# A fused expert MLP and prefix-softmax pooling kernel: the last batch's attention tail reordered, W's exponentials moved to ScalarE, and a batch's exponentials put in one place

## The chip, the cores and the metric

The kernel runs on one core of a Trainium2 chip. The metric is device time in microseconds (us) of one execution. Engines are named as in the profile: PE is TensorE (PEld its weight loads), DVE is VectorE, ACT is ScalarE, POOL is GpSimd, SP is SyncE, which issues the DMAs.

## The reference

Four batches of 1024 rows by 512. First a layer with a shared and an expert part, then attention pooling over all rows of a batch with a mask that depends on the batch's type. Both are added to x:

```python
h = gelu(x @ fc1_w.T + fc1_b)                     # exact gelu, 2048 hidden
y = concat(h @ fc2_w.T + fc2_b, h @ experts_w[idx].T + experts_b[idx])
x = x + y
scores = tanh(x @ W1 + b1) @ v                    # per 512 rows as [B, S]
mask   = l <= j, l >= j or l != j                 # by type 0, 1, 2
p      = softmax(where(mask, scores[l], -1e30))   # over l, for each row j
x = x + (p @ x) / count(mask)                     # S = 1024 here
```

## The kernel before

x is held transposed, 128 rows of features by 512 tokens in a tile. Every product of full precision is made of three with operands split in a high and a low part (`three`, L764 to L767): ACT makes the high part (`hi`, L981), DVE subtracts it to get the low part (`lo`, L1263). fc1 of a batch runs as Strassen-like products P1 to P7 into the banks hA and hF, in eight steps p (0 to 7, two blocks of 128 hidden each), with fc2 (banks y) of its first 512 rows in between and three places k for other work. Then 16 steps u do fc2 of its second 512 rows.

There are three bodies: `first`, `loop` (run for batches 1 to 3, `b` in code) and `tail`. The attention of batch b-1 is done in the loop body of batch b, in pieces hung at the places (p, k) by the table `POST_P`; that of the last batch is the tail, after the last product of fc2. In the tail each engine goes through its tasks in an order written by hand: PE by `TAIL_ORDER`, ACT by `TAIL_ACT`, DVE by `TAIL_DVE`. Banks go round: two job banks j in the loop, all eight in the tail, a job taking the next one once its last reader has counted `bank_read` up. In a loop step DVE and ACT do the tasks of (p, 0) before they go on with the adds and gelus of the products; product P2 overwrites hF, and so waits for DVE's add of hF (L1458, semaphore `add_done`); the sequence on PE is P1, P5, P6, jobs, P3, P7, jobs, P2, P4, with groups of fc2 between.

The attention of a batch, by task:

- `xn` transposes x back, four tiles a half (L858); ACT copies the high part, DVE subtracts; in the tail ACT also makes a full copy (`full`, counted by `xfull_done`) that the output is added to.
- `attn` is the product with W1, tanh by ACT (L1106), `score` the product with v (L866), s in an 8x128 layout (8 chunks of 128 rows).
- `maxima` scans s from both sides (L1424, L1426), `stats` (L870 to L872) transposes and spreads them; `row_maxima` (L1431 to L1440) makes Ef, t88, mc and the row maxima m8, of which `mT` (L876) and `bc` (L882, two of 512 columns) spread the negated maxima over 128 partitions.
- DVE adds scores and masks to them: P (own chunk, L1333, four of 128x128) and W (other chunks, L1337, one of 128x512) for each half. ACT takes the exponentials of both in place (L1147), then the high parts Ph and Ws (L981), DVE the low parts Pl and a third of Ws (L1263).
- `expE` spreads exp(Ef) on the diagonals of E4 (L1345), `sums` multiplies E4 with all of x (L887, L888: 16 products) to Bs.
- `scan`, `total`, `den`, `rd` make the denominators, with POOL (L705 to L717) and the small exponentials `exps_B` and `exps_M`.
- `pool` c: three products with Ph and Pl (`own_chunk`) and one of Ws with Bs (L904), DVE scales and adds (L1399 in the tail), SP stores. In the tail the own chunks of 0 to 3 are made before `rd` (L895).

Six fill products (L948, `FILLS`) stand in the tail's wait before `mT`. The tasks `expPW`, `exp` and `PW` are the exponentials of P and W and their split. Waits on the full copies, before their banks are written again, come from one table:

```python
FULL_BEFORE = {("bc", 0): 1, ("bc", 1): 2, ("sums",): 3, ("rd", 0, CH): 4}
```

## Time and profile before

| what | value |
|---|---|
| median of 3 runs | 784.71 us (783.61 to 785.57) |
| the profiled execution's own time | 784.57 us |
| its span, first to last instruction | 782.8 us |
| PE, DVE, ACT, POOL busy | 770.2, 402.5, 387.0, 132.7 us |
| mean granted clock of PE | 0.995 |
| last product of fc2 starts | 749.65 us |

Times within the profile are microseconds from the span's start. Busy time of PE has modelled ends: products of 512 columns show 0.39 us each and start 0.23 us apart at full clock, so starts are to be compared, not ends. "Granted clock" is the share of full speed (2.4 GHz) that the throttle gave PE. Between the end of the last instruction and the profiled execution's own time lie 1.8 us that the change doesn't touch. A group such as `x4` in a timeline is four instructions merged into one row.

### The profile page before, as it was taken

The numbers are of one execution on the slowest core, as the hardware profiler recorded it, in microseconds if no ns is written. First come the engines' busy times: TensorE is split into PE (matmuls) and PEld (weight loads), VectorE is DVE, ScalarE is ACT, GpSimd is POOL, SyncE is SP. The second block draws the span as 40 slices with busy tenths as digits, with TensorE's granted clock in tenths as the row PEclk, the third lists the DMA queues.
The fourth block names the chain that finished last, engine by engine and source line by source line (L and its number), as shares of the span: only waits on it lengthen the run. The fifth ranks groups of instructions, "written<-read, shape, count | busy, mean of one in ns | idle before, by whom it ended". The sixth has DMA issues, their size and how long they took to land.

```text
span 782.8 us, 11478 instructions
## 1 busy us (share of the span) xinstructions
PE 770.2 (98%) x3462; PEld 626.9 (80%) x3462; DVE 402.5 (51%) x713; ACT 387.0 (49%) x665; POOL 132.7 (17%) x184
## 2 busy tenths in 40 slices
PE   9999999999999999999999999999999999999977
PEld 6788888888888888888888888888887888888865
DVE  6854667563445332754536433376245542255666
ACT  6856665443546433543546633446254653344552
POOL 3172221400011121410001022050001102114011
PEclk9999999999999999999999999999999999999998
DMA  6899998877854568867776466985787466787722
GB/s 215 281 346 330 307 338 271 268 228 231 236 190 149 175 204 280 259 202 239 225 228 188 147 209 216 284 253 178 232 252 219 144 194 207 223 284 208 228 67 108
DMA packets 130715, 176.93 MB, mean 226 GB/s; under 512 B 10064, under 2 KB 97632, under 8 KB 130656
## 3 DMA queue, kind: packets, MB, share of 16 engines
q1 hardware_dynamic: 130496, 176.20, 72.0%
q8 instruction: 29, 0.48, 0.2%
q14 instruction: 30, 0.25, 0.1%
q0 software_dynamic: 160, 0.01, 0.0%
HBM read 136.33 MB, written 39.85 MB: 225 GB/s over the span
## 4 chain that ended last, share of the span: by engine, by line
PE 95%; DVE 2%; ACT 1%; DMA 1%; issue 0%; SPq 0%; DVEq 0%; ACTq 0%
PE y L765 15%; PE y L767 15%; PE y L766 15%; PE hA L765 8%; PE hA L767 7%; PE hA L766 7%; PE hF L765 6%; PE hF L766 6%; PE hF L767 5%; PE j L858 2%; PE j L765 1%; PE j L767 1%; PE j L766 1%; PE j L866 1%; PE j L835 1%; PE j L834 1%
## 5 line engine op out<-in xcount | busy, mean ns | idle before, releaser
L765 PE MATMUL y<-hs,w2c 128*128 128x512 f32 x512 | 201.8, 394 | 0.2
L767 PE MATMUL y<-hs,w2c 128*128 128x512 f32 x512 | 199.6, 390 | 0.0
L766 PE MATMUL y<-hs,w2c 128*128 128x512 f32 x512 | 199.4, 389 | 0.0
L765 PEld LDWEIGHTS y<-hs,w2c 128*128 128x128 f32 x512 | 96.1, 188 | 22.1 <-DVE hs L1263 1.9
L767 PEld LDWEIGHTS y<-hs,w2c 128*128 128x128 f32 x512 | 96.1, 188 | 20.5
L766 PEld LDWEIGHTS y<-hs,w2c 128*128 128x128 f32 x512 | 96.2, 188 | 19.3
L765 PE MATMUL hA<-xch,w1c 128*128 128x512 f32 x252 | 100.0, 397 | 0.9 <-DVE xcl L1263 0.6
L767 PE MATMUL hA<-xch,w1c 128*128 128x512 f32 x252 | 98.6, 391 | 0.0
L766 PE MATMUL hA<-xcl,w1c 128*128 128x512 f32 x252 | 98.6, 391 | 0.0
L1035 ACT ACTIVATE hst<-hst,bcol 128x512 f32<-128x512 f32 x62 | 43.9, 721 | 85.3 <-DVE hst L1458 85.3
L1263 DVE TENSOR_TENSOR hs<-gb,hs 128x512 fp32r<-128x512 f32 x64 | 43.5, 716 | 65.1 <-ACT hs L981 65.1
L765 PE MATMUL hF<-xch,w1c 128*128 128x512 f32 x190 | 76.2, 401 | 0.3 <-issue 0.3
L766 PE MATMUL hF<-xcl,w1c 128*128 128x512 f32 x190 | 74.5, 392 | 0.0
L767 PE MATMUL hF<-xch,w1c 128*128 128x512 f32 x190 | 74.3, 391 | 0.0
L1263 DVE TENSOR_TENSOR hs<-hst,hs 128x512 fp32r<-128x512 f32 x64 | 44.6, 697 | 37.3 <-ACT hs L981 36.2
L981 ACT ACTIVATE hs<-hst 128x512 fp32r<-128x512 f32 x64 | 40.4, 631 | 47.2 <-PE y L767 46.8
L765 PEld LDWEIGHTS hA<-xch,w1c 128*128 128x128 f32 x252 | 47.5, 188 | 13.9 <-issue 1.9
L767 PEld LDWEIGHTS hA<-xch,w1c 128*128 128x128 f32 x252 | 47.6, 189 | 10.1
L766 PEld LDWEIGHTS hA<-xcl,w1c 128*128 128x128 f32 x252 | 47.6, 189 | 9.4
L755 POOL TENSOR_TENSOR x1T<-x1T,xnl 128x512 f32<-128x512 f32 x24 | 30.8, 1290 | 137.9 <-DVE x1T L1402 137.9
L1458 DVE TENSOR_TENSOR hst<-hF,hst 128x512 f32<-128x512 f32 x31 | 21.4, 691 | 56.4 <-PE hF L767 55.9
L1035 ACT ACTIVATE gb<-gb,bcol 128x512 f32<-128x512 f32 x31 | 22.4, 724 | 54.8 <-DVE gb L1458 54.7
(283 smaller groups left out, 1096.3 us busy)
## 6 DMA issues: line engine op xcount, KB each, us to landing
w2c<-w2s SPq DMA_DIRECT2D x114, 384.0 KB, 3.5
w1c<-w1s SPq DMA_DIRECT2D x24, 768.0 KB, 4.6
w2c<-exs SPq DMA_DIRECT2D x114, 128.0 KB, 4.0
w1c<-w1s SPq DMA_DIRECT2D x48, 256.0 KB, 3.5
w1c<-w1s SPq DMA_DIRECT2D x24, 512.0 KB, 4.1
x1T<-in_x SPq DMA_DIRECT2D x32, 256.0 KB, 5.6
w1s<-w1c SPq DMA_DIRECT2D x8, 768.0 KB, 4.4
w2s<-w2c SPq DMA_DIRECT2D x16, 384.0 KB, 4.5
```

What stands on the lines that cost most here:

```text
L755: nc.gpsimd.tensor_tensor(oo[:, c % OUTS, :], oo[:, c % OUTS, :], xnl[:, c, :].bitcast(f32), ALU.add).then_inc(row_sum, 1)
L765: nc.tensor.matmul(ps, ah, bh, start=first, stop=False, skip_group_check=onto)
L766: nc.tensor.matmul(ps, ah, bl, start=False, stop=False, skip_group_check=onto)
L767: return nc.tensor.matmul(ps, al, bh, start=False, stop=last, skip_group_check=onto)
L834: nc.tensor.matmul(bank[:, :], W1h[:, dc, :], xh[:, dc, :], start=dc == 0, stop=False)
L835: nc.tensor.matmul(bank[:, :], W1l[:, dc, :], xh[:, dc, :], start=False, stop=False)
L858: last = nc.tensor.transpose(bank[:, i * P:(i + 1) * P], x1T[:, i, c * P:(c + 1) * P], ident[:, :])
L866: last = nc.tensor.matmul(bank[0:CH, 0:P], vz[:, t * CT + i, :], th[t][:, i * P:(i + 1) * P], start=(i == 0), stop=(i == CT - 1))
L981: return nc.scalar.activation(out_, in_, ACT.Copy)
L1035: nc.scalar.activation(tile, hA[:, :] if order == 4 else tile, ACT.Gelu, bias=bcol[:, R_FC1 + m:R_FC1 + m + 1]).then_inc(gelu_done, 1)
L1263: return nc.vector.tensor_tensor(out_, in_, hi_.bitcast(f32), ALU.subtract)
L1458: nc.vector.tensor_tensor(tile, bank[:, :], tile, ALU.add).then_inc(add_done, 1)
```

## The change

- In the tail, `attn` goes ahead of xn 1, its tanh comes in two halves (own semaphore), the score product ahead of xn 3; `total` behind `sums`; one fill product fewer, and they don't wait for a full copy.
- The three operations of the row maxima that only need the own chunk (m0) go from `row_maxima` to `maxima`, that is from behind `stats` to ahead of it, in all batches; Ef behind mc. A new small operation makes Wb, the bias of W.
- DVE no longer adds W: ACT takes W's exponentials straight from the bank of bc, four of 128x128 a half with Wb as bias, into the same tile. The bank is then free when ACT has read it, not DVE.
- In a loop body both halves of the exponentials stand at (3, 0), where the second half stood at (4, 0); at (4, 0) only its split is left.
- In the tail, ACT and DVE do P and W apart, in a new order, and the last full copy is ACT's last task; the waits for full copies move.
- E4 gets 8 columns more so that the three casts to its diagonals become one.

The tables and PE's part:

```diff
-WARM, FILLS = 8, 6
+WARM, FILLS = 8, 5
...
-          (2, 2): [("mT",)], (3, 0): [("bc", 0), ("bc", 1), ("expE",), ("expB",), ("expM",), ("scan",), ("expPW", 0)],
+          (2, 2): [("mT",)], (3, 0): [("bc", 0), ("bc", 1), ("expE",), ("expB",), ("expM",), ("scan",), ("exp", 0), ("exp", 1), ("split", 0)],
           (3, 1): [("sums",), ("total",)], (3, 2): [("den",)],
-          (4, 0): [("rd", 0, BC), ("rd", BC, CH), ("expPW", 1)], (4, 1): [("pool", 0)], (4, 2): [("pool", 1)],
+          (4, 0): [("rd", 0, BC), ("rd", BC, CH), ("split", 1)], (4, 1): [("pool", 0)], (4, 2): [("pool", 1)],
...
-    ("xn", 0), ("xn", 1), ("attn",), ("xn", 2), ("xn", 3), ("score",), ("stats",), ("expE",), ("mT",), ("bc", 0), ("bc", 1),
-    ("scan",), ("total",), ("expPW", 0), ("expPW", 1), ("sums",), ("den",), ("rd", 0, CH)] + [("pool", c) for c in range(CH)]
+    ("xn", 0), ("attn",), ("xn", 1), ("xn", 2), ("score",), ("xn", 3), ("stats",), ("expE",), ("mT",), ("bc", 0), ("bc", 1),
+    ("scan",), ("split", 0), ("split", 1), ("sums",), ("total",), ("den",), ("rd", 0, CH)] + [("pool", c) for c in range(CH)]
...
-    ("xn", 0), ("xn", 1), ("attn",), ("xn", 2), ("xn", 3), ("full", 0), ("full", 1), ("expE",), ("expB",), ("full", 2), ("expM",),
-    ("full", 3), ("exp", 0), ("PW", 0), ("exp", 1), ("sums",), ("PW", 1)]
+    ("xn", 0), ("attn",), ("xn", 1), ("xn", 2), ("full", 0), ("xn", 3), ("expE",), ("full", 1), ("expB",), ("full", 2),
+    ("splitP", 0), ("expM",), ("splitW", 0), ("splitP", 1), ("sums",), ("splitW", 1), ("full", 3)]
...
-            ("xn", 1), ("score",), ("xn", 2), ("stats",), ("mT",), ("expE",), ("xn", 3), ("bc", 0), ("scan",), ("bc", 1),
-            ("expPW", 0), ("total",), ("sums",), ("expPW", 1), ("den",), ("rd", 0, CH)] + [("pool", c) for c in range(CH)]
-
-FULL_BEFORE = {("bc", 0): 1, ("bc", 1): 2, ("sums",): 3, ("rd", 0, CH): 4}
+            ("xn", 1), ("score",), ("xn", 2), ("stats",), ("mT",), ("expE",), ("bcP", 0), ("xn", 3), ("scan",),
+            ("loP", 0), ("bcP", 1), ("loW", 0), ("total",), ("sums",), ("loP", 1), ("den",), ("loW", 1), ("rd", 0, CH)] + [("pool", c) for c in range(CH)]
+
+FULL_BEFORE = {("bc", 0): 1, ("sums",): 2, ("total",): 3, ("pool", 0): 4}
...
-                    wait_used(pe, kind, b, at(kind, place, ("attn",)))
+                    if kind == "tail":
+                        pe.wait_ge(tanh_half, 1)
+                    else:
+                        wait_used(pe, kind, b, at(kind, place, ("attn",)))
                     if kind == "first":
                         pe.wait_ge(vz_done, 1)
                     for i in range(CT):
+                        if kind == "tail" and i == CT // 2:
+                            wait_used(pe, kind, b, at(kind, place, ("attn",)))
...
-                    wait_used(pe, kind, b, at(kind, place, ("xn", CT - 1)))
                     for c in range(CH):
+                        if c >= CT:
+                            wait_used(pe, kind, b, at(kind, place, ("xn", c - CT)))
...
 
                             idle = jb[bank_of(kind, at(kind, "p", ("bc", 1)))]
-                            pe.wait_ge(xfull_done, FULL_BEFORE["bc", 1])
                             for i in range(FILLS):
                                 nc.tensor.matmul(idle[:, :], W1h[:, 0, :], x1he[:, 0, :], start=True, stop=True)
...
                             pe.wait_ge(xfull_done, FULL_BEFORE[task])
 
                         for c in range(BC) if task[0] == "rd" else [task[1]] if task[0] == "pool" and task[1] >= BC else []:
+                            if ("pool", c) in FULL_BEFORE:
+                                pe.wait_ge(xfull_done, FULL_BEFORE["pool", c])
```

ACT's part:

```diff
-                    nc.scalar.activation(th[t], bank[:, :], ACT.Tanh, bias=bcol[:, R_B1:R_B1 + 1]
-                                         ).then_inc(bank_read[bank_of(kind, pos)], 1)
+                    if kind == "tail":
+                        mid = TT // 2
+                        nc.scalar.activation(th[t][:, 0:mid], bank[:, 0:mid], ACT.Tanh, bias=bcol[:, R_B1:R_B1 + 1]).then_inc(tanh_half, 1)
+                        nc.scalar.activation(th[t][:, mid:], bank[:, mid:], ACT.Tanh, bias=bcol[:, R_B1:R_B1 + 1]
+                                             ).then_inc(bank_read[bank_of(kind, pos)], 1)
...
-                    split_PW(kind, b, task[1])
+                    exp_P(b, task[1])
+                    exp_W(kind, b, place, task[1])
+                elif task[0] == "split":
+                    split_PW(kind, b, task[1], 0)
+                    split_PW(kind, b, task[1], 1)
+                elif task[0] == "splitP":
+                    exp_P(b, task[1])
+                    split_PW(kind, b, task[1], 0)
+                elif task[0] == "splitW":
+                    exp_W(kind, b, place, task[1])
+                    split_PW(kind, b, task[1], 1)
...
-            def exp_PW(kind, b, place, h):
+            def exp_P(b, h):
                 half = slice(h * TT, (h + 1) * TT)
-                wait_used(act, kind, b, at(kind, place, ("bc", h)))
-                for tile in (Pf, Wf):
-                    nc.scalar.activation(tile[:, half], tile[:, half], ACT.Exp).then_inc(exp_done, 1)
-
-            def split_PW(kind, b, h):
+                act.wait_ge(P_in, b * 2 + (h - 1))
+                nc.scalar.activation(Pf[:, half], Pf[:, half], ACT.Exp).then_inc(exp_done, 1)
+
+            def exp_W(kind, b, place, h):
+
+                pos = at(kind, place, ("bc", h))
+                bank = jb[bank_of(kind, pos)]
+                act.wait_ge(P_in, b * 2 + (h - 1))
+                for i in range(CT):
+                    c = h * CT + i
+                    last = nc.scalar.activation(Wf[:, c * P:(c + 1) * P], bank[:, i * P:(i + 1) * P], ACT.Exp, bias=Wb[:, c:c + 1])
+                last.then_inc(bank_read[bank_of(kind, pos)], 1)
+                wait_used(act, kind, b, pos)
+                act.sem_inc(exp_done, 1)
...
-                for i, (part_, full) in enumerate(((Ph, Pf), (Ws, Wf))):
-                    act.wait_ge(exp_done, b * 5 + (2 * h + i - 3))
-                    hi(part_[:, cs, :].rearrange("p c n -> p (c n)"), full[:, half]).then_inc(PWhi, 1)
+                part_, full = ((Ph, Pf), (Ws, Wf))[i]
+                act.wait_ge(exp_done, b * 5 + (2 * h + i - 3))
+                hi(part_[:, cs, :].rearrange("p c n -> p (c n)"), full[:, half]).then_inc(PWhi, 1)
```

DVE's part (`link` waits for its own instruction; `split_P` and `split_W` are the two subtractions that stood under `expPW`):

```diff
-                elif task[0] == "bc":
+                elif task[0] in ("bc", "bcP"):
 
                     for i in range(CT):
                         c = task[1] * CT + i
-                        nc.vector.scalar_tensor_tensor(Pf[:, c * P:(c + 1) * P], bank[:, i * P:(i + 1) * P], st[:, c:c + 1],
-                                                       TM[:, TRI], ALU.add, ALU.add)
-                    half = slice(task[1] * TT, (task[1] + 1) * TT)
-                    cross = TM[:, P + task[1] * CT:P + (task[1] + 1) * CT]
-                    nc.vector.scalar_tensor_tensor(
-                        Wf[:, half].rearrange("p (c n) -> p c n", c=CT), bank[:, :].rearrange("p (c n) -> p c n", c=CT),
-                        st[:, 2 * CH:2 * CH + 1], cross.unsqueeze(2).to_broadcast([P, CT, P]), ALU.add, ALU.add
-                    ).then_inc(used, 1)
+                        last = nc.vector.scalar_tensor_tensor(Pf[:, c * P:(c + 1) * P], bank[:, i * P:(i + 1) * P], st[:, c:c + 1],
+                                                              TM[:, TRI], ALU.add, ALU.add)
+                    last.then_inc(P_in, 1)
                 elif task[0] == "expE":
-                    diagonal = E4[:, :, :].rearrange("p c n -> p (c n)")
...
-                        last = nc.vector.tensor_copy(diagonal[:, 32 * gr:32 * gr + (CH - 1) * (P + 1) + 1:P + 1], Ef[:, :])
-                    last.then_inc(Ehi, 1)
+                    nc.vector.tensor_copy(groups[:, :, 0:32 * (GROUPS - 1):32], Ef[:, :].unsqueeze(2).to_broadcast([P, CH, GROUPS - 1])
...
+                link(nc.vector.scalar_tensor_tensor(m0[:, :], G8[:, 1:P + 1], TM[0:CH, NP_:NP_ + 1], m0[:, :],
+                                                    ALU.add, ALU.max), b, 5)
+                nc.vector.scalar_tensor_tensor(m0[:, :], F8[:, 0:P], TM[0:CH, NS:NS + 1], m0[:, :], ALU.add, ALU.max
+                                               ).then_inc(chain, 1)
+
             def row_maxima(b):
 
+                link(nc.vector.tensor_tensor(t88[:, :], st[0:CH, CH:2 * CH], TM[0:CH, SEEN], ALU.add), b, 7)
+                link(nc.vector.reduce_max(mc[:, :], t88[:, :], AX.X), b, 8)
                 nc.vector.tensor_tensor(Ef[:, :], st[:, 0:CH], st[:, CH:2 * CH], ALU.subtract).then_inc(chain, 1)
-                link(nc.vector.tensor_tensor(t88[:, :], st[0:CH, CH:2 * CH], TM[0:CH, SEEN], ALU.add), b, 5)
-                nc.vector.reduce_max(mc[:, :], t88[:, :], AX.X).then_inc(chain, 1)
-                link(nc.vector.tensor_scalar(m0[:, :], s8[:, :], TM[0:CH, NC:NC + 1], None, ALU.add), b, 7)
-                link(nc.vector.scalar_tensor_tensor(m0[:, :], G8[:, 1:P + 1], TM[0:CH, NP_:NP_ + 1], m0[:, :],
-                                                    ALU.add, ALU.max), b, 8)
-                link(nc.vector.scalar_tensor_tensor(m0[:, :], F8[:, 0:P], TM[0:CH, NS:NS + 1], m0[:, :],
-                                                    ALU.add, ALU.max), b, 9)
                 nc.vector.tensor_scalar(m8[:, :], m0[:, :], mc[:, :], -1.0, ALU.max, ALU.mult).then_inc(chain, 1)
                 nc.vector.tensor_scalar(t88[:, :], t88[:, :], mc[:, :], None, ALU.subtract).then_inc(chain, 1)
+
+                nc.vector.tensor_scalar(Wb[:, :], TM[:, CROSS], st[:, 2 * CH:2 * CH + 1], None, ALU.add)
 
```

How it moves instructions, at three places. First ACT at step 3 of a loop body, from the last small exponential to the gelu; x1T is the tile that holds P and W, j the bank. Before:

```order
L1141 ACTIVATE s8a<-m,mc 8x128
L1147 ACTIVATE x1T<-x1T 128x512 [waits bank_read0]
L1147 ACTIVATE x1T<-x1T 128x512
...
L981 ACTIVATE Ph<-x1T 128x512 [waits exp_done]
L981 ACTIVATE Ws<-x1T 128x512 [waits exp_done]
...
L1035 ACT_TABLE_LOAD
L1035 ACTIVATE hst<-hst,bcol 128x512 [waits add_done]
```

With the change:

```order
L1164 ACTIVATE s8a<-m,mc 8x128
L1169 ACTIVATE x1T<-x1T 128x512 [waits P_in]
L1178 ACTIVATE x1T<-j,Wb 128x128 [waits P_in]
L1178 ACTIVATE x1T<-j,Wb 128x128 x3
...
L1169 ACTIVATE x1T<-x1T 128x512 [waits bank_read0,P_in]
L1178 ACTIVATE x1T<-j,Wb 128x128 [waits P_in]
L1178 ACTIVATE x1T<-j,Wb 128x128 x3
...
L993 ACTIVATE Ph<-x1T 128x512 [waits exp_done]
...
L993 ACTIVATE Ws<-x1T 128x512 [waits exp_done]
...
L1047 ACT_TABLE_LOAD
L1047 ACTIVATE hst<-hst,bcol 128x512 [waits add_done]
```

Two exponentials of 128x512 stood ahead of the copy to Ph; two of 128x512 and eight of 128x128 stand there now.

Second PE in the tail, from the second broadcast to the first own chunk. Before:

```order
L882 MATMUL j<-ident,mT 128x128 [waits bank_read7,bank_read1,xfull_done]
L892 MATMUL hA<-DG,ones 8x8 [waits den_scan,bank_read2]
L887 MATMUL hF<-xnh,E 128x512 [waits Elo,bank_read4,bank_read3,xfull_done]
L888 MATMUL hF<-xnl,E 128x512
...
L765 MATMUL y<-xnh,Ph 128x512 [waits Plo,bank_read5,xfull_done]
L766 MATMUL y<-xnl,Ph 128x512
L767 MATMUL y<-xnh,Pl 128x512
```

With the change:

```order
L890 MATMUL j<-ident,mT 128x128 [waits bank_read7,bank_read1]
L896 MATMUL hA<-xnh,E 128x512 [waits Elo,bank_read2,xfull_done]
L897 MATMUL hA<-xnl,E 128x512
...
L896 MATMUL hA<-xnh,E 128x512 [waits bank_read0]
...
L901 MATMUL hF<-DG,ones 8x8 [waits den_scan,bank_read3,xfull_done]
L768 MATMUL y<-xnh,Ph 128x512 [waits Plo,bank_read5,xfull_done]
L769 MATMUL y<-xnl,Ph 128x512
L770 MATMUL y<-xnh,Pl 128x512
```

The product of `total` (DG) went from ahead of the sums to behind them; the sums went to another bank. The first own chunk waits for all four full copies (`xfull_done` at 4), as before.

Third ACT at the end of the tail, from the exponentials of P's first half on; hst is the full copy. Before:

```order
L981 ACTIVATE hst<-y 128x512 [waits bank_read4]
L1147 ACTIVATE x1T<-x1T 128x512 [waits bank_read0]
L1147 ACTIVATE x1T<-x1T 128x512
L981 ACTIVATE Ph<-x1T 128x512 [waits ex_in,exp_done,exlo,ex_out0]
L981 ACTIVATE Ws<-x1T 128x512 [waits exp_done]
L1147 ACTIVATE x1T<-x1T 128x512 [waits bank_read1]
L1147 ACTIVATE x1T<-x1T 128x512
L981 ACTIVATE Bs<-hF 128x512 [waits job_done]
L981 ACTIVATE Ph<-x1T 128x512 [waits ex_in,exp_done,exlo,ex_out1]
L981 ACTIVATE Ws<-x1T 128x512 [waits exp_done]
```

With the change:

```order
L1169 ACTIVATE x1T<-x1T 128x512 [waits P_in]
L993 ACTIVATE Ph<-x1T 128x512 [waits ex_in,exp_done,exlo,ex_out0]
...
L1178 ACTIVATE x1T<-j,Wb 128x128 [waits P_in]
L1178 ACTIVATE x1T<-j,Wb 128x128 x3
L993 ACTIVATE Ws<-x1T 128x512 [waits bank_read0,ex_in,exp_done,exlo,ex_out0]
L1169 ACTIVATE x1T<-x1T 128x512 [waits P_in]
L993 ACTIVATE Ph<-x1T 128x512 [waits ex_in,exp_done,exlo,ex_out1]
L993 ACTIVATE Bs<-hA 128x512 [waits job_done]
...
L993 ACTIVATE Ws<-x1T 128x512 [waits bank_read1,ex_in,exp_done,exlo,ex_out1]
L993 ACTIVATE hst<-y 128x512 [waits bank_read5]
```

The last full copy went from ahead of all large exponentials to the end of the queue; the four small exponentials of `exps_M` stand in the first gap.

## Rows read from the trace of the kernel before

**Rows 1.** Page, busy time, share of the span, instructions of each engine

```profile
PE 770.2 (98%) x3462; PEld 626.9 (80%) x3462; DVE 402.5 (51%) x713; ACT 387.0 (49%) x665; POOL 132.7 (17%) x184
```

**Rows 2.** Waits of PE over the span: us in total, times, longest us

```profile
PE hA L892 <- DVE DG L1371: 2.9, 1, 2.9
```

**Rows 3.** Timeline of PE, step 3 of a batch: start us, us, instruction

```profile
233.44 1.03 PE L882 MATMUL j<-ident,mT 128*128 128x128 f32 x8
...
238.43 0.39 PE L887 MATMUL j<-xnh,E 128*128 128x512 f32 x1
...
242.28 0.50 PE L765 MATMUL hF<-xch,w1c 128*128 128x512 f32 x1
...
247.87 0.39 PE L765 MATMUL hA<-xch,w1c 128*128 128x512 f32 x1
...
422.91 1.03 PE L882 MATMUL j<-ident,mT 128*128 128x128 f32 x8
```

**Rows 4.** Timeline of ACT, the same stretch

```profile
236.57 0.39 ACT L1141 ACTIVATE s8a<-m,mc 8x128 f32<-8x128 f32 x1
236.86 1.14 ACT L1147 ACTIVATE x1T<-x1T 128x512 f32<-128x512 f32 x2
237.91 0.61 ACT L981 ACTIVATE Ph<-x1T 128x512 fp32r<-128x512 f32 x1
...
239.06 1.28 ACT L1035 ACT_TABLE_LOAD   x1
```

**Rows 5.** Timeline of DVE, the same stretch

```profile
238.69 0.67 DVE L1263 TENSOR_TENSOR Pl<-x1T,Ph 128x512 fp32r<-128x512 f32 x1
239.39 1.12 DVE L1263 TENSOR_TENSOR Ws<-x1T,Ws 32x512 fp32r<-32x512 f32 x1
240.54 0.69 DVE L1458 TENSOR_TENSOR hst<-hF,hst 128x512 f32<-128x512 f32 x1
```

**Rows 6.** Timelines of ACT, DVE and PE at step 4 of that batch

```profile
253.45 1.28 ACT L1147 ACT_TABLE_LOAD   x1
...
257.88 0.69 DVE L1458 TENSOR_TENSOR hst<-hF,hst 128x512 f32<-128x512 f32 x1
...
259.06 0.39 PE L765 MATMUL hF<-xch,w1c 128*128 128x512 f32 x1
```

**Rows 7.** Timeline of DVE in the tail

```profile
755.53 0.28 DVE L1319 TENSOR_TENSOR s<-y,s8a 8x128 f32<-8x128 f32 x1 [1.05 <-PE y L866]
...
757.35 0.15 DVE L1323 COPY st<-y 128x17 f32<-128x17 f32 x1
757.99 0.25 DVE L1431 TENSOR_TENSOR Ef<-st 128x8 f32<-128x8 f32 x1 [0.49 <-DVE st L1323]
...
759.10 0.34 DVE L1437 SCALAR_TENSOR_TENSOR m<-FG,TM,m 8x128 f32<-8x128 f32 x1
759.47 0.27 DVE L1439 TENSOR_SCALAR m<-m,mc 8x128 f32<-8x128 f32 x1
...
779.20 0.75 DVE L1399 SCALAR_TENSOR_TENSOR hst<-y,rd,hst 128x512 f32<-128x512 f32 x1
```

**Rows 8.** Timeline of PE in the tail

```profile
760.53 1.06 PE L882 MATMUL j<-ident,mT 128*128 128x128 f32 x8 [0.35 <-DVE mT L1328]
...
764.68 0.76 PE L887 MATMUL hF<-xnh,E 128*128 128x512 f32 x1
...
768.63 0.40 PE L888 MATMUL hF<-xnl,E 128*128 128x512 f32 x1
...
770.23 0.39 PE L765 MATMUL y<-xnh,Ph 128*128 128x512 f32 x1
...
773.70 0.35 PE L895 MATMUL y<-ident,m 8*128 8x8 f32 x2 [0.59 <-DVE m L1382]
```

**Rows 9.** Timeline of ACT in the tail, its last row

```profile
771.44 0.62 ACT L981 ACTIVATE Ws<-x1T 128x512 fp32r<-128x512 f32 x1
```

**Rows 10.** Stretches: us, busy PE PEld DVE ACT POOL, granted clock, DMA

```profile
762.00:764.00 2.00, 0.00 (x0) 0.00 (x0) 2.00 (x7) 0.90 (x2) 0.00 (x0) 0.50 0.00 0
```

More of the change, by code:

```diff
@@ L238, in build @@
         Q8 = sb("Q8", [CH, 1])
+        Wb = sb("Wb", [P, CH])
         DG = sb("DG", [CH, CH])
@@ L940, in part @@
                             fc2(kind, b, n, oc)
-                    attn(kind, b, "p", range(DC - 1), at(kind, "p", ("attn",)))
+                    first = at(kind, "p", ("attn",))
+                    pe.wait_ge(bank_read[bank_of(kind, first)], bank_turn(kind, b, first))
+                    attn(kind, b, "p", range(DC - 1), first)
                     for task, pos in TAIL["p", 0, 0]:
@@ L1105, in task_part @@
                         act.wait_ge(hslo, units(b, HC - 2, 1, 1))
-                    nc.scalar.activation(th[t], bank[:, :], ACT.Tanh, bias=bcol[:, R_B1:R_B1 + 1]
-                                         ).then_inc(bank_read[bank_of(kind, pos)], 1)
+                    if kind == "tail":
[3 more added lines that the diff above has]
+                                             ).then_inc(bank_read[bank_of(kind, pos)], 1)
+                    else:
+                        nc.scalar.activation(th[t], bank[:, :], ACT.Tanh, bias=bcol[:, R_B1:R_B1 + 1]
+                                             ).then_inc(bank_read[bank_of(kind, pos)], 1)
                 elif task[0] == "expE":
@@ L1210, in part @@
                     for task in TAIL_ACT:
-                        task_part(kind, b, "p", task, at(kind, "p", task) if task[0] not in ("full", "exp", "PW", "expB", "expM") else 0)
+                        task_part(kind, b, "p", task, at(kind, "p", task) if task[0] not in ("full", "splitP", "splitW", "expB", "expM") else 0)
                     return
@@ L1268, in task_part @@
                 bank, used = jb[bk], bank_read[bk]
-                if task[0] in ("score", "stats", "mT", "bc", "total", "rd", "pool"):
+                if task[0] in ("score", "stats", "mT", "bc", "bcP", "total", "rd", "pool"):
                     dve.wait_ge(job_done, job_of(kind, b, pos) + 1)
@@ L1403, in task_part, with split_P, split_W @@
                                                    ALU.mult, ALU.add).then_inc(used, 1)
+            def split_P(b, h):
+                half, cs = slice(h * TT, (h + 1) * TT), slice(h * BC, (h + 1) * BC)
+                dve.wait_ge(PWhi, b * 4 + (2 * h - 3))
+                lo(Pl[:, cs, :].rearrange("p c n -> p (c n)"), Pf[:, half], Ph[:, cs, :].rearrange("p c n -> p (c n)")
+                   ).then_inc(Plo, 1)
+            def split_W(b, h):
+                half, cs = slice(h * TT, (h + 1) * TT), slice(h * BC, (h + 1) * BC)
+                dve.wait_ge(PWhi, b * 4 + (2 * h - 2))
+                third = Ws[64:96, cs, :].rearrange("p c n -> p (c n)")
+                lo(third, Wf[64:96, half], third).then_inc(Wlo, 1)
             def sum_of_x(b, k, x_):
```

45 lines of the change are left out of this document (21 added, 24 removed).

## The prediction

> **What bounds the kernel now.** I read the page first: PE is busy for 98% of the span [rows 1]. Then the waits of PE: its longest is 2.9 us, before L892, for DVE [rows 2], and apart from some before 10 us all lie in the tail (another stands before L895, 0.59 [rows 8]). So in the three loop bodies PE never waits, and every us that something there makes it wait is added to the time; in the tail, after 749.9 us, a chain over all engines sets the end. Last the timelines of both places. One profiled execution is the base: it took 784.57 us with a span of 782.8, and the median of the runs is 784.71, so I predict against 784.57.
>
> **Loop, step 3 of a pair.** PE makes the columns bc at 233.44, starts the sums at 238.43 and the product P2 into hF at 242.28, back to back with its other products [rows 3]. P2 overwrites hF, so it waits for DVE's add of hF to hst, which runs at 240.54 for 0.69 us, to 241.23 [rows 5]: slack 1.05 us. DVE's queue sets that add: it comes behind the subtractions for Pl and Ws, and those wait for ACT's copies Ph and Ws [rows 4, 5]. ACT begins the large exponentials at 236.86 and the copies at 237.91: two of 128x512 in 1.05, 0.525 each [rows 4].
>
> The change gives ACT more to do ahead of these copies, and makes W's exponentials four each. A 128x128 exponential with a bias column out of the bank is not in the trace. Bounds: a quarter of 0.525, 0.13 us, if only elements count; 0.39, a full one of 8x128 with a bias column, if none overlap. The nearest row is such a short exponential, and the one after it starts 0.29 behind it [rows 4]; I take 0.29. Then:
> - P's first half from 236.86 to 237.39 (next start); four of W to 238.55, the last ends at 238.65. Only now is bc's first bank free, which sums needs: 0.3 us behind PE's 238.43 (before, DVE freed it long before).
> - ACT waits for its own end (taken as 0.1, from 0 to 0.2), then P's second half at 238.75, W's from 239.28 to 240.54, again 0.1, Ph at 240.65 to 241.26, Ws to 241.78. Before, Ph began at 237.91: 2.74 later.
> - DVE: Pl's subtraction at 241.32 (before 238.69), Ws's at 242.0. That took 1.12, beside a POOL sum that now falls earlier (the scan no longer stands behind two large W additions), so 0.68, as at step 4. The add starts at 242.72 and ends at 243.41.
> - P2 can start at 243.47 instead of 242.28: PE stalls 1.19 us, the 0.3 of the sums within it.
>
> Further down nothing is late: by the same counting ACT's fourth gelu ends near 248.5, and the next P1, which waits for it, comes at 247.87 [rows 3] + 1.19 = 249.06. The batches show the same times 189.5 us apart (233.44 and 422.91 [rows 3]), so the loop costs 3 x 1.19 = **3.6 us**. With 0.13 per short exponential the stall is 1.19 - 8 x 0.16, none; with 0.39 it is 2.0, 6.0 in all.
>
> **Loop, the rest.** DVE's own part of the maxima, three operations of 0.3 to 0.4, moves from (2, 1) to (2, 0); the queue behind them there holds no large exponentials, and the add ends before its P2, so I cost it at nothing; its cover is the time of PE's products P3 and P7, and without it up to 1 us a batch would show. DVE loses W's two additions and two of three casts: off PE's path except as used above. At step 4 ACT loses two exponentials and two table loads (to exp and back to gelu). The load takes 1.28 us [rows 6]. DVE's add there ends at 257.88 + 0.69 = 258.57, before P2 at 259.06 [rows 6]: PE did not wait, so I cost the gain at nothing. The Trainium skill, "ScalarE: Activation LUTs", section "Table sets: the hidden batching unit", says to group activations by table set, at about 2.7 us for each switch. By it six switches fewer would be worth some 16 us, an estimate from that page.
>
> SP's queue and POOL's order stay as they are; the zeros of E at the start grow from 512 to 520 columns, hidden.
>
> **Tail, to the broadcast.** The transposes xn 1 go behind attn, and tanh comes in halves: the scores are done 0.5 us sooner. But DVE now has xnl of tile 1 ahead of its s, behind an ACT copy that stands behind both tanhs; s starts at about 755.14 instead of 755.53 [rows 7], 0.4 sooner. The three operations of the own maxima then precede xnl 2 (0.97: one to the next takes 0.37, from 759.10 to 759.47 [rows 7], the first two somewhat less), so the statistics are copied at 757.94, not 757.35; after that t, mc, Ef and m8 take 0.68 to m8's start at 758.62 instead of 759.47 [rows 7], a gain of 0.85 (only 0.4, if the 0.49 us of idle at 757.99, behind that copy [rows 7], returns).
>
> **Tail, sums and own chunks.** bc follows m8 by 1.06, as now (759.47, then 760.53) [rows 7, 8]. sums no longer waits for total and starts at 760.65, not at 764.68; at full clock its 16 products end at 764.4, not at 770.4 [rows 8]. Taken alone this is up to 4 us.
>
> It isn't alone. The own chunks of pool 0 to 3 wait, as before, for the fourth full copy, and that copy is now the last thing in ACT's tail. ACT's queue, with its starts: P's first half 761.43 (bc 0 added by DVE at 761.38), Ph 762.08, four small exponentials from 762.60, W from 763.79, Ws 765.12, P's second half 765.64, Ph 766.29, Bs 766.81, W from 767.33, Ws 768.67, the full copy 769.20 to 769.80. That is: seven of 0.52, two waits of 0.13 within, twelve short ones of 0.29 and two self-waits of 0.17: 7.7 us, up to the start of the full copy. Before, ACT's last row began at 771.44 [rows 9], but PE had run its own chunks from 770.23 without it [rows 8]. PE starts them at 769.87, a gain of only 0.36.
>
> **The clock.** PE then sat idle from 764.6 to 769.87, 5.3 us. In the trace, little work on PE before 762 and none until 764.45 came with a granted clock of 0.50, which is 1.2 GHz of 2.4 [rows 10]; nine steps of products then took 764.68 to 768.63, 0.43 each, and it returned to full; the rest ran at 0.23 [rows 8]. Twelve products of own chunks so take 3.95 + 3 x 0.23 = 4.64 us, and the reciprocal's column L895 comes at 774.5 instead of 773.70: 0.8 **later**. DVE's eight output rows follow at their own rate as now, to 779.20 + 0.75 [rows 7]. The tail costs 0.8.
>
> **Sum.** 784.57 + 3.6 + 0.8 = **789.0 us**.
>
> **Rivals.** What this kernel's measurement can tell from no change is 0.3%, 2.35 us, so slower begins at 787.06 and faster below 782.36.
> - *The clock holds, or comes back at once, in the own chunks*: 12 x 0.23 = 2.76, L895 at 772.6, 1.1 sooner: 784.57 + 3.6 - 1.1 = 787.0. For it: sums keeps PE dense to 764.4; against: 5.3 us idle is longer than the idle that went with 0.50. Chance 0.20, half of it on either side of 787.06.
> - *Half clock lasts longer*, into the last four chunks, of four products each at 0.43, 1.7 us where DVE takes at most 0.75 per row [rows 7]: L895 at 775.0 and 0.5 more: tail 1.9, 790.1. Chance 0.12.
> - *Short exponentials overlap* (the other side): at 0.14 us or less each, eight at step 3 cost what two did, and P2 never stalls. In the tail the full copy ends 1.2 us sooner: with half clock 784.1 (chance 0.06), with full clock L895 is 2.4 sooner: 782.2 (0.05). Against it: the 0.29 of rows 4, with only 8 partitions but the same 128 columns.
> - *Table loads on the path*: if ACT at step 4 holds PE in a way that the waits hide, six loads of 1.28 go: 776.9. Against it stands the slack of 0.49 in rows 6. This is the rule of the table sets in the Trainium skill. Chance 0.03.
> - *The stall is absorbed*, or the delay doesn't reach PE: only the tail counts, 785.4. PE has no idle to absorb it. Chance 0.04.
> - My forecast: 0.50.
>
> **Numbers.** The range, 785.4 to 792.0, leaves out the last two cases of the short exponentials and the table loads (0.14) and some 0.05 above; its top is 0.39 per short exponential (2.4 more in the loop, near 1 in the tail less what the slack takes). Slower by over 0.3%: 0.50 + 0.12 + 0.10 = 0.72. Within: 0.10 + 0.06 + 0.04 = 0.20. Faster: 0.05 + 0.03 = 0.08.
>
> **What would show it.** In the changed profile: PE waits three times before P2 of step 3 for DVE's add of hF, 0.9 us, and three times before sums for ACT, 0.3; loop bodies 190.7 apart, not 189.5; one pair of table loads a batch; four W exponentials 0.29 apart; sums in the tail near 760.7 + 3.6; PE idle for 5 us until ACT's last copy, then products at 0.43. I am wrong in kind if PE shows no wait at step 3, or if the own chunks start well before ACT's last copy.

## The result, and the profile after

The changed kernel takes **790.45 us** (median of 6 runs, 789.61 to 793.07); the kernel before, beside it, 784.12 (6 runs, 783.41 to 785.57): ratio 1.0083, 95% interval 1.0072 to 1.0093. The profiled execution took 790.58 us with a span of 788.9, against 784.57 and 782.8. It is slower, as forecast, and 1.5 us beyond the 789.0 given.

The page first; PE is still busy for 98% [rows 1]:

```profile
span 788.9 us, 11501 instructions
PE 771.8 (98%) x3461; PEld 626.5 (79%) x3461; DVE 401.6 (51%) x701; ACT 382.9 (49%) x684; POOL 125.6 (16%) x184
```

Then the waits of PE (us in total, times, longest). The 2.9 us for DG [rows 2] are gone, and two others stand in their place: one before the own chunks, and three in the loop, where there had been none. The wait for m8 before `mT` grew from 1.0 to 1.3 us; its row of before comes last.

```profile
PE y L768 <- ACT hst L993: 4.5, 1, 4.5
PE hF L768 <- DVE hst L1498: 2.7, 3, 0.9
PE y L884 <- DVE m L1477: 1.3, 1, 1.3
```

```profile
PE y L876 <- DVE m L1439: 1.0, 1, 1.0
```

Step 3 of a batch, first ACT, then DVE, then PE (start us, us, instruction), which answer to [rows 3 to 5]. These bodies start 1.35 us earlier than those of before, at 232.09 against 233.44.

```profile
235.23 0.39 ACT L1164 ACTIVATE s8a<-m,mc 8x128 f32<-8x128 f32 x1
235.52 0.61 ACT L1169 ACTIVATE x1T<-x1T 128x512 f32<-128x512 f32 x1
236.04 1.09 ACT L1178 ACTIVATE x1T<-j,Wb 128x128 f32<-128x128 f32 x4
237.25 0.63 ACT L1169 ACTIVATE x1T<-x1T 128x512 f32<-128x512 f32 x1
237.79 1.12 ACT L1178 ACTIVATE x1T<-j,Wb 128x128 f32<-128x128 f32 x4
239.18 0.63 ACT L993 ACTIVATE Ph<-x1T 128x512 fp32r<-128x512 f32 x1 [0.27 <-ACTq L1181]
```

```profile
239.84 0.69 DVE L1297 TENSOR_TENSOR Pl<-x1T,Ph 128x512 fp32r<-128x512 f32 x1 [3.87 <-ACT Ph L993]
240.57 0.68 DVE L1297 TENSOR_TENSOR Ws<-x1T,Ws 32x512 fp32r<-32x512 f32 x1
241.28 0.69 DVE L1498 TENSOR_TENSOR hst<-hF,hst 128x512 f32<-128x512 f32 x1
```

```profile
232.09 1.03 PE L890 MATMUL j<-ident,mT 128*128 128x128 f32 x8
...
237.18 0.50 PE L896 MATMUL j<-xnh,E 128*128 128x512 f32 x1
...
241.03 0.20 PE L901 MATMUL j<-DG,ones 8*8 8x8 f32 x2
242.12 0.47 PE L768 MATMUL hF<-xch,w1c 128*128 128x512 f32 x1 [0.89 <-DVE hst L1498]
```

From bc (232.09) the copy Ph stands 7.09 us behind; before it was 4.47 (237.91 - 233.44). DVE idles 3.87 us for it, the add of hF follows at once, and P2 comes 10.03 behind bc instead of 8.84: **1.19 us of stall**. Of it 0.89 is the wait; the rest is lost at the sums (the product ahead of them began 0.34 earlier instead of 0.23, and L901 behind them comes at 8.94 from bc, not 8.71) and at the restart.

The tail starts with the first product of `attn`: L834 at 749.87 in the kernel before (first line), L837 at 752.80 in the changed one. PE, then DVE, then ACT, to be read beside [rows 7 to 9]:

```profile
749.87 0.39 PE L834 MATMUL hA<-x1e,W1h 128*128 128x512 f32 x1
```

```profile
752.80 0.39 PE L837 MATMUL j<-x1e,W1h 128*128 128x512 f32 x1
...
763.25 1.94 PE L890 MATMUL j<-ident,mT 128*128 128x128 f32 x8 [0.35 <-DVE mT L1361]
...
764.84 0.78 PE L896 MATMUL hA<-xnh,E 128*128 128x512 f32 x1
...
774.14 0.80 PE L768 MATMUL y<-xnh,Ph 128*128 128x512 f32 x1 [4.54 <-ACT hst L993]
...
779.56 0.59 PE L904 MATMUL y<-ident,m 8*128 8x8 f32 x2
```

```profile
762.19 0.27 DVE L1477 TENSOR_SCALAR m<-m,mc 8x128 f32<-8x128 f32 x1
...
764.37 1.13 DVE L1366 SCALAR_TENSOR_TENSOR x1T<-j,st,TM 128x128 f32<-128x128 f32 x4 [0.61 <-PE j L890]
...
780.69 2.07 DVE L1423 SCALAR_TENSOR_TENSOR hst<-y,rd,hst 128x512 f32<-128x512 f32 x3
```

```profile
765.53 0.63 ACT L1169 ACTIVATE x1T<-x1T 128x512 f32<-128x512 f32 x1 [1.35 <-DVE x1T L1366]
...
773.51 0.58 ACT L993 ACTIVATE hst<-y 128x512 f32<-128x512 f32 x1
```

The sums do come forward, to 12.04 us behind the tail's start (752.80; before 764.68 - 749.87 = 14.81), and PE then waits 4.54 us for ACT's last copy. The half clock is there already in bc: its eight products take 1.94 us instead of 1.06 [rows 8], and DVE starts on P 1.12 us behind bc's start, where in the repeat of the same kernel (e10, below) it starts 0.66 behind. The own chunks run at half clock, as the stretches show (us, busy PE PEld DVE ACT POOL, granted clock, DMA); compare [rows 10]:

```profile
762.00:764.00 2.00, 1.14 (x6) 1.08 (x7) 1.49 (x8) 1.69 (x6) 1.08 (x2) 0.76 0.00 0
764.00:766.00 2.00, 2.00 (x9) 1.81 (x8) 1.63 (x5) 0.65 (x2) 0.00 (x0) 0.50 0.00 0
...
774.00:776.00 2.00, 1.86 (x4) 1.49 (x5) 0.32 (x1) 0.09 (x1) 0.00 (x0) 0.50 0.00 0
776.00:778.00 2.00, 2.00 (x6) 1.59 (x5) 0.00 (x0) 0.00 (x0) 0.00 (x0) 0.50 0.00 0
778.00:780.00 2.00, 2.00 (x6) 1.16 (x5) 0.00 (x0) 0.00 (x0) 0.00 (x0) 0.50 0.03 8
```

All runs can be laid side by side if the span is cut at three rows that every kernel has: the first bc of the loop, the first product of `attn` that opens the tail (L834 before, L837 in the changed kernel), and DVE's first output row. This table does so from the timelines, in us; "body" is bc to bc, "own" the first own chunk counted from the tail's start, and the four stages without "body" and "own" add up to the span.

```text
kernel            start   loop   (body)   tail  (own)   end    span
before            233.44 516.43  189.47  24.71  20.36   8.22  782.8
after             232.09 520.71  190.89  27.89  21.34   8.21  788.9
e10 (after again) 233.08 520.78  190.91  26.33  20.89   8.21  788.4
e1_old_loop       233.03 517.25  189.71  26.62  21.23   9.90  786.8
e2_split_first    232.59 518.07  190.00  25.45  21.57   9.89  786.0
e3_full_early     233.02 520.82  190.90  22.48  16.83   8.48  784.8
e4_keep_busy      232.47 520.70  190.90  25.27  21.54   8.16  786.6
e5_both           232.37 518.13  190.01  22.53  16.81  10.07  783.1
e6_pool_later     233.75 520.81  190.92  26.13  20.41   9.91  790.6
e11 (e6 again)    232.36 520.76  190.90  25.97  20.40   8.21  787.3
e7_both_pool      233.94 518.13  190.01  21.57  14.73   8.86  782.5
e9_old_full       232.87 517.22  189.72  21.86  14.71   8.55  780.5
e12_fill_gap      233.23 517.22  189.71  21.85  14.73   8.20  780.5
e13_aligned       233.40 516.40  189.45  21.86  14.73   8.54  780.2
```

For the change it reads: start -1.35, loop +4.28, tail +3.18, end -0.01: +6.1, the difference of the spans. The forecast had loop +3.6 and tail +0.8. Start and end are not the kernel's: the same code differs there from run to run (below).

### The profile page after: what moved, and what is told of

Its sections match the earlier page's. It is cut to its first block, busy times and chain, and to the rows that moved or that the text cites. A ratio compares the mean times of both kernels' runs of the same rounds, so it can differ in the third digit from the quotient of the medians.

```text
span 788.9 us, 11501 instructions
## 1 busy us (share of the span) xinstructions
PE 771.8 (98%) x3461; PEld 626.5 (79%) x3461; DVE 401.6 (51%) x701; ACT 382.9 (49%) x684; POOL 125.6 (16%) x184
## 4 chain that ended last, share of the span: by engine, by line
PE 89%; ACT 5%; DVE 2%; issue 2%; DMA 1%; SPq 1%; ACTq 0%; DVEq 0%
PE y L768 15%; PE y L770 14%; PE y L769 14%; PE hA L768 7%; PE hA L770 7%; PE hA L769 7%; PE hF L768 5%; PE hF L770 5%; PE hF L769 5%; PE j L861 2%; ACT x1T L1178 1%; PE j L840 1%; PE j L838 1%; PE j L837 1%; PE j L874 1%
```

## The experiments

All start from the changed kernel. The kernel before, on the same chips, took 784.40 us beside e1 to e4, 784.77 beside e5, e6, e7 and e9, 784.96 beside e10 to e12, and 784.48 beside e13.

### The loop: put back, or split first

**e1_old_loop** puts back DVE's additions of W and two full-size exponentials, the second pair at (4, 0):

```diff
-(3, 0): [..., ("scan",), ("exp", 0), ("exp", 1), ("split", 0)]
+(3, 0): [..., ("scan",), ("expPW", 0)]
-(4, 0): [..., ("split", 1)]
+(4, 0): [..., ("expPW", 1)]
```

> The loop bodies go back to the old way for the exponentials (DVE adds W, ACT takes the second half at step 4); the maxima's new order and the tail stay changed. Theory Q (ACT's longer queue at step 3 makes PE wait at P2): the 1.2 us stall of each batch goes and, if it hangs on the same move, the slow drift of 0.25 a batch too: 790.4 - 3 x 1.4 = 786.2, loop bodies 189.5 apart. Rival M (the own maxima, moved ahead in every batch, cost the loop its time): nothing changes, 790.4. The tail alone then stands at about +2 over before.

Measured 788.54 (787.40 to 789.43), ratio 1.0050 (1.0037 to 1.0063). PE's wait for the add is gone, and the bodies are 189.71 apart: 1.18 of the 1.42 us a body, 3.46 over the loop. The slow drift of 0.25 a body stayed, and the median gave back only 1.9 us, where 4.2 had been expected. In the trace, set against e10's with nearly the same start and tail, the loop is 3.5 us shorter and the end 1.7 longer (9.90 instead of 8.21); whether the other four executions ended late too, no trace shows.

**e2_split_first** changes one word: P's first half is split before the second half's exponentials.

```diff
-("exp", 0), ("exp", 1), ("split", 0)
+("exp", 0), ("split", 0), ("exp", 1)
```

> The change, but at step 3 of a loop body the copies Ph and Ws of the first half stand between the two halves' exponentials, on ACT and DVE. Theory Q: Ph starts some 1.7 us sooner, DVE's add of hF is ready before P2, and of the stall only the 0.25 at sums is left, which waits for ACT to read the bank: 790.4 - 3 x 0.95 = 787.6. Rival B (it is the reading of the bank by ACT that costs, wherever the copies stand): 790.4.

Measured 789.26 (787.74 to 791.83), ratio 1.0067 (1.0053 to 1.0080). The median is only 1.2 us below the change's, not the 2.8 expected, and the two intervals overlap: by the times alone this run is not told from the change. The trace tells more (the profiled execution was the fastest of the six):

```profile
232.59 0.60 PE L890 MATMUL j<-ident,mT 128*128 128x128 f32 x4
```

```profile
241.68 0.50 PE L768 MATMUL hF<-xch,w1c 128*128 128x512 f32 x1
```

P2 comes 9.09 behind bc, without a wait, and the bodies are 190.00 apart: the 0.89 before P2 are gone, and 0.25 stay at the sums, since W's first four exponentials still stand between bc and the release of its bank. So the stall has the two parts that the forecast gave it, and the order of ACT's queue makes the larger.

### The tail: ACT's last copy, and the clock

**e3_full_early** moves the fourth full copy ahead of the small exponentials.

```diff
-("splitP", 0), ("expM",), ("splitW", 0), ("splitP", 1), ("sums",), ("splitW", 1), ("full", 3)
+("splitP", 0), ("full", 3), ("expM",), ("splitW", 0), ("splitP", 1), ("sums",), ("splitW", 1)
```

> The change, but the fourth full copy stands behind the first splitP in ACT's tail, not at its end. Theory F (PE's own chunks wait for that copy, 4.5 us, and then run at half clock): PE goes from sums and total at 769.4 straight to the own chunks at full clock, done at 772.3; L904 then waits for the denominators, near 774 instead of 779.6: 790.4 - 5.4 = 785.0. Rival C (PE would only wait for something else as late, Plo or the denominators behind ACT's queue): under 1 us, 789.6 or more.

Measured 786.40 (785.65 to 788.51), ratio 1.0028 (1.0018 to 1.0037): 4.0 us less than the change, though 1.4 more than expected. The own chunks start at 16.83 instead of 21.34 and the pooling 5.4 sooner. The wait for ACT is gone from PE's waits, and L904 waits 1.3 us for the totals instead:

```profile
PE y L904 <- DVE m L1406: 1.3, 1, 1.3
```

**e4_keep_busy** leaves the order as it is and puts 20 idle products, whose results nothing reads, into the gap before the own chunks.

> The change with 20 more fill products between total and the own chunks, into the bank of rd; the output is the same. They take PE through 4.5 of the idle time, the copy stays last. Theory K (the half clock of the own chunks costs 2.7 us and comes from the idle time before them): granted clock 1.00 there, twelve products in 2.7, not 5.4, and L904 at full clock: 790.4 - 2.9 = 787.5. Rival: the clock was low already for what lies before (bc and the first sums ran at half clock), and the fills change nothing: 790.4.

Measured 788.38 (788.29 to 790.10), ratio 1.0058 (1.0045 to 1.0070). The own products run 0.23 apart, the twelve of them in 2.81 us instead of 5.42 (PE's timeline):

```profile
774.71 0.39 PE L768 MATMUL y<-xnh,Ph 128*128 128x512 f32 x1
774.94 0.39 PE L769 MATMUL y<-xnl,Ph 128*128 128x512 f32 x1
...
777.52 0.38 PE L904 MATMUL y<-ident,m 8*128 8x8 f32 x2
```

So the half clock comes from the idle before them, and costs up to 2.6 us (the median fell by 2.1, against 2.9 expected). How much of it an execution pays varies with the tail's code unaltered: from the first own product to L904 it took 5.42 us (after), 4.52 (e10), 4.47 (e1) and 2.96 (e2), behind an idle of 4.5, 4.0, 4.3 and 3.4. e2 paid nearly nothing, and its idle was the shortest, as its sums had run longer at half clock. But the idle's length alone doesn't set the price: in e6 below it was 5.6, and they took 4.81.

**e5_both** joins e2 and e3.

> Two edits together: in the loop the first half of P is split before W's exponentials of the same half, in the tail the full-size copy of the last chunks goes ahead of the maxima's copy and of W's split. Theory (the two costs lie in different places and add): 0.9 us of the 1.2 us stall in each of three batches goes (2.7 us), and the tail ends 4 to 5.5 us sooner as in the run with the copy alone; by the medians of the two single runs 790.4 - 1.2 - 4.0 = 785.2, by their traces 790.4 - 2.7 - 4.0 = 783.7. Rival (the end of the span is set by something behind the arithmetic, as the two runs with a changed loop ended 9.9 us after the last pooling instead of 8.2): 785.2 or more, with the pooling itself at the place the theory says.

Measured 783.90 (782.40 to 784.82, 12 runs), ratio 0.9990 (0.998 to 1.000). Body 190.01 and tail 22.53 are those of e2 and e3: the costs add. By the traces they add to 783.7, by the medians to 785.2; the measured median is the one by the traces. The profiled execution, the slowest of the twelve, ended late too.

### GpSimd beside VectorE

**e6_pool_later** lets GpSimd's first denominators wait for the sixth step of DVE's chain, the last of the own maxima, and no longer for the two scans (`BOTH`).

```diff
-gate(pool, chain, b * NCHAIN + (BOTH - NCHAIN))
+gate(pool, chain, b * NCHAIN + (6 - NCHAIN))
```

> GpSimd's first denominators of a batch wait until VectorE has written its own maxima, where they started beside them. Theory (the two small VectorE operations on the maxima took 0.74 and 0.58 us instead of 0.34 each because GpSimd's operations ran beside them on the shared path to SBUF): both come back to about 0.35 us, the maxima of the last batch are ready 0.6 us sooner, and the time falls to about 789.8 us. Rival (they are slow for a reason of their own, such as the operands' place): their durations stay at 0.6 to 0.7 us and the time stays at 790.4.

Measured 792.34 (790.95 to 792.62), 1.9 **above** the change: both theories missed. The two operations did what was expected. In the changed kernel (DVE, then POOL):

```profile
759.65 0.74 DVE L1467 SCALAR_TENSOR_TENSOR m<-FG,TM,m 8x128 f32<-8x128 f32 x1
760.43 0.58 DVE L1469 SCALAR_TENSOR_TENSOR m<-FG,TM,m 8x128 f32<-8x128 f32 x1
```

```profile
759.62 0.63 POOL L708 TENSOR_TENSOR FS<-s,FG 8x256 f32<-8x256 f32 x1 [43.09 <-DVE m L1466]
760.22 0.65 POOL L709 TENSOR_TENSOR decay<-FG 8x256 f32<-8x256 f32 x1
```

and with GpSimd later:

```profile
761.42 0.34 DVE L1467 SCALAR_TENSOR_TENSOR m<-FG,TM,m 8x128 f32<-8x128 f32 x1
761.79 0.34 DVE L1469 SCALAR_TENSOR_TENSOR m<-FG,TM,m 8x128 f32<-8x128 f32 x1
```

```profile
762.31 0.64 POOL L708 TENSOR_TENSOR FS<-s,FG 8x256 f32<-8x256 f32 x1 [44.02 <-DVE m L1469]
```

The tail was 26.13 against 27.89. But the loop began 1.66 us later (233.75) and the end was 1.7 longer. That asked for the same two kernels again, on one chip: **e10_change_again** and **e11_pool_again**.

> The changed kernel again, nothing altered. It is here to stand on the same chip as the next run. Theory (2 us of every execution are decided by its first 10 us, where the first loads land and where the half-clock stretch falls, and 1.7 us by whether the last instruction fetch of TensorE's queue falls among the output stores): its median lies within 789.6 to 792.3, not exactly at 790.4, and in its trace the first broadcast product of the second batch starts between 232.0 and 234.0. Rival (both are fixed by the kernel's code): 790.4 with the first broadcast at 232.1 and the end 8.2 us after the first pooling.

> The kernel with GpSimd's later start again, which in its first run was 1.9 us slower than the change's own median although its tail, counted from the first attention product to the first pooling, was 1.8 us shorter. Theory (the tail is shorter every time, start and end are chance): the tail is again 26.1 us against 27.9, and the median lies 0.5 to 1.8 us below that of the run before on the same chip. Rival (GpSimd's later start costs something at the start or at the end, every time): the median is again 1 to 2 us above it.

Measured 790.46 (789.52 to 790.97) and 790.43 (788.98 to 792.29). So the 1.9 is not the edit's: the same code gave 792.34 on one chip and 790.43 on another, and whether the chip or chance made the difference was not tried. And much of what a single profile shows of the start is not the code's either: the change's loop began at 233.08 here, not at 232.09, and its tail took 26.33, not 27.89. GpSimd's later start gives 0.36 us by this pair (26.33 to 25.97), and the medians don't show it; the 0.5 to 1.8 expected was too much, taken from the one profile with the longest half clock.

**e7_both_pool** puts it on e5.

> The two edits of the run before with GpSimd's later start added. Theory: another 0.6 us off the tail, 783.1 us by the traces or 784.6 by the medians. Rival (the clock level in the tail decides more than the queue's order): the broadcast and the own chunks run at half clock in this run or in that one, and the two times differ by up to 2 us without a relation to the edit.

Measured 783.13 (781.92 to 785.26, 12 runs), ratio 0.9982 (0.9972 to 0.9992): 0.8 less than e5, as its trace said (the tail is 1.0 shorter), and the 783.1 of the theory. The intervals of e5 and e7 overlap, so the 0.8 rests on the traces more than on the medians. Here the sums are on the path, and they start 10.76 us into the tail where they had started at 12.03. That pattern has no exception: in the six traces with GpSimd later they start at 10.76 to 10.78; in the seven others with the new tail, where m8 comes 0.49 later and PE waits 1.3 us for it instead of 0.8, at 11.46 to 12.25.

### A version that beats both, and the last quarter microsecond

**e9_old_full** is e1, e3 and e6 together.

> The loop's exponentials as they were before the change (W added by VectorE, two full-size exponentials, then the splits), the tail's full-size copy ahead of the maxima's, and GpSimd's later start. Theory: the stall of 1.2 us per batch is gone (3.6 us), the tail gains 4 to 5 us and 0.6 us: 790.4 - 3.6 - 4.0 - 0.6 = 782.2 us, 783.9 with the late end that the two runs with a changed loop showed; both lie below the kernel before (784.4). Rival (the remaining 0.25 us per batch and the longer tail of the new order keep it behind): 785 us or more.

Measured 782.72 (781.63 to 784.65, 12 runs), ratio 0.9975 (0.9964 to 0.9986): a quarter of a percent faster than the kernel before. The new tail, with its copy early and GpSimd later, is 2.85 us shorter than the old one (21.86 against 24.71).

**e12_fill_gap** adds nine idle products before L904, to e9.

> The fastest version so far (the loop's old exponentials, the tail's full copy early, GpSimd later) with nine idle products on TensorE in the 2.5 us in which it waited for the totals, between the own chunks of the first three and the totals of the last. Theory (the wait lets the clock fall to half, and ten of the sixteen products behind it then take 0.43 us instead of 0.23): all sixteen run 0.23 apart, the last pooling is no longer held by them and ends 0.5 to 0.8 us sooner, so about 782.1 us against 782.7. Rival (VectorE's pooling, eight operations of 0.66 us one behind the other, sets the end whatever the clock): 782.7 and the last pooling no sooner.

Measured 782.71 (781.64 to 784.72, 12 runs): no gain by the median. All products behind the totals run 0.23 apart, and DVE's last row starts 26.47 us into the tail and not 27.04. So the theory was right about that row, the rival about the time: in e9 DVE's last two rows had still waited 0.16 and 0.18 us for PE. More is not to be had there, as the pooling begins at 21.85 as before and DVE's eight rows, 0.66 apart, set the pace. The end after it is 0.35 us shorter in this trace and the start 0.36 longer, and the spans are equal; a gain of half a us is not told apart by twelve executions on either side.

All versions so far, e1 and e9 too, had bodies about 0.25 longer than before, beside any stall. Aligned row by row, the difference builds up between 25 and 65 us behind bc, where PE never waits. The groups of PE's products in that stretch (257 to 300 us; busy us, mean ns of one), before and in e9:

```profile
L767 PE MATMUL hF<-xch,w1c 128*128 128x512 f32 x14 | 5.4, 389 | 0.0
L904 PE MATMUL j<-Bs,Ws 128*128 128x512 f32 x8 | 3.1, 389 | 0.0
```

```profile
L770 PE MATMUL hF<-xch,w1c 128*128 128x512 f32 x14 | 5.5, 395 | 0.0
L913 PE MATMUL j<-Bs,Ws 128*128 128x512 f32 x8 | 3.2, 398 | 0.0
```

**e13_aligned** is e9 with the tiles behind E on other addresses.

```diff
-E4f = sb("E4", [P, CH * (P + 1)], f32r)
+E4f = sb("E4", [P, CH * (P + 16)], f32r)[:, 0:CH * (P + 1)]
-Wb = sb("Wb", [P, CH])
 ...
 rd = sb("rd", [P, CH])
+Wb = sb("Wb", [P, CH])
```

> The version with the loop's old exponentials, the early full copy and GpSimd's later start, and one thing more: the change made the tile E 32 bytes longer and put a small tile of eight columns among the others, which moved all tiles behind them by 32 or 64 bytes per partition; here E is followed by a gap so that they lie 512 bytes further than before the change, and the small tile comes last. It is to tell where the 0.25 us per batch come from that every new version carries (bodies 189.71 apart against 189.47) and that build up over 40 us of products behind step 4 without any wait. Theory (where the tiles lie): the bodies are 189.45 to 189.5 apart again and the time is 0.75 us less, 782.0. Rival (the order of the instructions in the queues): 189.71 and 782.7.

Measured **781.88** (781.44 to 782.51), ratio 0.9962 (0.9949 to 0.9976), the fastest. Its interval overlaps e9's, on another chip, so the main evidence is the trace: bodies 189.45 apart, no drift against before in the whole stretch, and both groups back at their old means:

```profile
L770 PE MATMUL hF<-xch,w1c 128*128 128x512 f32 x14 | 5.4, 389 | 0.0
L913 PE MATMUL j<-Bs,Ws 128*128 128x512 f32 x8 | 3.1, 389 | 0.0
```

The order of instructions, the rival, is that of e9. So it was where the tiles lie: the change made E 32 bytes longer and put Wb between others. Which tile it is was not tried, nor why the place matters; Bs, an operand of the product at 398 ns, lies right behind E.

## Why the prediction was right, and where it was off

- **Loop stall: right in mechanism, place and size.** 1.19 forecast, 1.19 measured, three times; e1 and e2 remove it whole and in its larger part. That it agrees to the hundredth is luck of small errors. A short exponential starts 0.25 behind the one before, not 0.29 (0.32 less in all), and ACT's wait for its own end before Ph is 0.27, not 0.1, so that Ph came 0.12 earlier than forecast; P2 then started 0.15 behind the end of DVE's add, not 0.06, and DVE's steps took the rest. The rival with overlapping short exponentials (0.14 or less each) is refuted.
- **What the loop term missed** is 0.23 us a body, +4.28 over the loop instead of +3.6. The step that failed is "Loop, the rest", priced at nothing: I counted what E's 520 columns cost to clear, and not that they and Wb move other tiles. e13, where the 0.25 is gone with the tiles put elsewhere, shows it.
- **Table loads: worth nothing.** One pair a batch is left, as said (9 loads instead of 15), and no time came back: e1 loads the tables 15 times again, and its bodies are shorter than the change's by the stall (1.18) and no longer for the loads. The Trainium skill, "ScalarE: Activation LUTs", section "Table sets: the hidden batching unit", by which six switches fewer would save some 16 us as an estimate, is not borne out by this trace: a load takes 1.28 us in it, and PE does not wait for ScalarE at step 4.
- **Own maxima in the tail: 0.64 late.** m8 comes 9.39 behind the tail's start, against 9.60 before: a gain of 0.21, where the forecast had 0.85, or 0.4 with the idle. The failed step is the price of L1467 and L1469, taken from a lone row as 0.3 to 0.37; beside GpSimd they took 0.74 and 0.58. e6 brought them back to 0.34 and m8 to 8.91.
- **Sums: start at 12.04 instead of 10.78.** Of the 1.26 us 0.64 is the later m8; the rest came because the clock fell right behind PE's wait for m8, near 763.0 (0.76 in the stretch of 762 to 764), so that bc ran at half clock. The forecast had the half clock in the own chunks alone. It reached further than the sums: bc's first columns came later to DVE, P to ACT, and so ACT's queue and the own chunks (0.46 us against e10).
- **Own chunks behind ACT's last copy: right.** The queue took 7.98 us, not 7.7, and began 12.73 us into the tail, not 11.56 (0.64 for m8, most of the rest for bc at half clock): own chunks at 21.34 instead of 20.0. e3 confirms the cause and makes it the largest single cost: 4.0 us by the medians, 5.4 by its trace against the changed kernel's and 3.9 against e10's.
- **Clock: right in kind.** All twelve own products at half in this profile, 5.42 to L904 against 4.64; 4.52 in the repeat. The same tail code also gave 2.96 (e2), near the rival "holds", and this run's 5.42 is at its rival "lasts longer" (775.0 - 769.87 = 5.1), so they were a spread and not alternatives.
- **The tail's term**, +0.8, measured +3.2 in the profiled run and +1.6 in e10. That is the term that was mis-sized. Of the 2.4 us too little in the profiled run, 1.34 are the later own chunks, 0.78 their longer half clock and 0.25 the step from L904, still at half clock, to DVE's first row. Loop and tail together came out 3.1 us above the forecast, and the start's -1.35, which no term of the forecast had, took 1.35 of them out of the sum: the 1.5 us by which the number missed is luck to that extent.

## What to carry to other kernels

Moving work to an idle engine moves its whole queue: look for the copy or release that stands last behind the new work, and put it first (one word moved in each of two lists was worth 2.6 us by the trace and about 4 by the medians here). Before pricing a small VectorE operation from a lone row, look what GpSimd does beside it, and before pricing an enlarged tile at nothing, look at what lies behind it. When stages are compared, cut the span at rows that all kernels share; medians of few runs and single profiles carry 2 us of start and end that belong to no edit.

## What was not expected of the hardware

- **Small VectorE operations beside GpSimd**: 8x128 with three inputs took 0.74 and 0.58 us while POOL operations of 8x256 ran, 0.34 without, in every trace of either kind, in the loop bodies as in the tail.
- **A tile's place**: products with the same shape and count took up to 395 (hF) and 398 ns (Bs, Ws) instead of 389 in a stretch without waits, and 389 again with the tiles 512 bytes off their old place (e13).
- **The start**: the same code reached the loop at 232.09 and 233.08 (e6 and its repeat at 233.75 and 232.36), and all kernels between 232.09 and 233.94. Part of it is where half clock falls in the first 12 us: products stood 0.43 apart from 5.4 to 10.5 us in the kernel before, and 0.23 apart from the first one in the changed one, whose first product had waited 1.05 us for DVE.
- **The end**: from the first output row to the end of the span it is 8.2 to 8.9 us in ten of the fourteen traces, and 9.9 to 10.1 in e1, e2, e5 and e6. In these four the last fetch of instructions of queue q8, one packet of 16 KB, falls among the output stores; in the ten it falls ahead of them or after. This is it in e6, from 786 to 788 us, where the store on the way took 4.0 us to land against 2.2 in the median of the eight:

```profile
q8 instruction: 1, 0.02, 3.0%
```

  e6 and its repeat are the same code, with 9.91 and 8.21. That the fetch causes the delay was not tried, only that the two come together.
